# Inverting 32x32 instead of 16x16 diagonal blocks on GpSimd before the doubling on TensorE

## The reference

```python
A = jnp.where(strict_lo, kb @ jnp.swapaxes(k, -1, -2), 0.0)
Tinv = jax.scipy.linalg.solve_triangular(eye + A, eye, lower=True, unit_diagonal=True)
u = Tinv @ v
w = Tinv @ kb
def step(S, xs):
    q_i, k_i, u_i, w_i = xs
    attn = jnp.where(strict_up, 0.0, q_i @ jnp.swapaxes(k_i, -1, -2))
    u_i = u_i - w_i @ S
    o_i = q_i @ S + attn @ u_i
    S = S + jnp.swapaxes(k_i, -1, -2) @ u_i
    return (S, o_i)
```

## Time and profile before

| what | value |
|---|---|
| median of the runs | 3596.17 us |
| the profiled execution, its span | 3601.86 us, 3600.1 us |
| PE busy, share of the span | 3078.8 us, 86% |
| DVE busy | 2413.5 us, 67% |
| ACT busy | 1393.4 us, 39% |
| POOL busy | 383.3 us, 11% |
| mean granted clock of PE | 0.884 of full speed |
| ordinary step that starts at 1554.64 us | 206.80 us |

### The profile page before, as it was taken

The page is one execution under the profiler, slowest core; times in us unless marked ns, Lnnn a source line. Parts: engine busy times, 40 slices in busy tenths (PEclk is TensorE's granted clock), DMA queues, the critical chain, the costliest instruction groups (busy, mean ns, idle before and its releaser), DMA issues.

```text
span 3600.1 us, 49639 instructions
## 1 busy us (share of the span) xinstructions
PE 3078.8 (86%) x18500; PEld 2342.5 (65%) x18500; DVE 2413.5 (67%) x5735; ACT 1393.4 (39%) x2889; POOL 383.3 (11%) x710
## 2 busy tenths in 40 slices
PE   4689899898989889898998989889898989988565
PEld 2467767676766767676676767667676766757352
DVE  5436677686867668686766768585676858675754
ACT  2344343534444253434434343443434344332311
POOL 1001010010102011010100101020010101020200
PEclk7699889898989989898998989899898989988666
DMA  3344253323334232333424233432432353231100
GB/s 103 74 100 118 42 115 71 82 67 88 81 87 97 59 91 65 82 80 87 100 57 103 67 76 71 106 80 57 104 76 69 69 105 81 54 89 45 34 14 20
DMA packets 592814, 275.94 MB, mean 77 GB/s; under 512 B 464808, under 2 KB 555072, under 8 KB 592576
## 3 DMA queue, kind: packets, MB, share of 16 engines
q1 hardware_dynamic: 490176, 138.53, 20.3%
q10 hardware_dynamic: 102400, 134.23, 12.6%
HBM read 156.55 MB, written 14.68 MB: 48 GB/s over the span
## 4 chain that ended last, share of the span: by engine, by line
PE 53%; DVE 24%; issue 6%; ACT 6%; DMA 4%; POOL 4%; SPq 2%; DVEq 0%; POOLq 0%; ACTq 0%
PE bank L906 20%; PE bank L1111 7%; DVE region L2000 6%; PE bank L981 4%; PE bank L958 3%; PE bank L941 3%; PE bank L1272 2%; ACT pt_f L1371 2%; PE bank L915 2%; DMA qT_f<-pt_f 2%; DVE nm_f L1738 2%; POOL region L884 1%; PE bank L1239 1%; PE bank L1204 1%; SPq L716 1%
## 5 line engine op out<-in xcount | busy, mean ns | idle before, releaser
L906 PE MATMUL bank<-xTc,c_w 128*128 128x256 f32 x2048 | 528.4, 405 | 3.2 <-DVE yc L1924 3.1
L1371 ACT ACTIVATE pt_f<-bank 128x512 f32<-128x512 f32 x768 | 419.1, 597 | 266.0 <-PE bank L958 262.9
L1111 PE MATMUL bank<-c_w,c_hb 128*128 128x256 f32 x2048 | 481.9, 384 | 2.8 <-ACT c_hb L1504 2.4
L906 PEld LDWEIGHTS bank<-xTc,c_w 128*128 128x128 f32 x2048 | 403.1, 206 | 71.5 <-issue 7.3
L1738 DVE TENSOR_REDUCE nm_f<-bank 128x2 f32<-128x512 f32 x512 | 316.3, 685 | 164.3 <-PE bank L941 162.1
L2000 DVE SCALAR_TENSOR_TENSOR region<-vpad,cols,region 128x256 f32<-128x256 f32 x1024 | 420.2, 485 | 0.0
L1111 PEld LDWEIGHTS bank<-c_w,c_hb 128*128 128x128 f32 x2048 | 377.3, 191 | 64.8 <-issue 11.1
L958 PE MATMUL bank<-qT_f,kT_f 102*128 102x256 bf16 (+1 forms) x1536 | 275.7, 296 | 65.8 <-ACT pt_f L1371 33.7
L1504 ACT ACTIVATE c_hb<-bank,cols 128x256 f32<-128x256 f32 x512 | 213.6, 476 | 303.5 <-PE bank L906 302.5
L958 PEld LDWEIGHTS bank<-qT_f,kT_f 102*128 102x128 bf16 (+1 forms) x1536 | 129.1, 101 | 219.9 <-ACT pt_f L1371 98.4
L981 PE MATMUL bank<-pt_f,v_f 128*32 128x256 f32 x3072 | 219.9, 419 | 0.0
(11 more groups left out here) (317 smaller groups left out, 5140.9 us busy)
## 6 DMA issues: line engine op xcount, KB each, us to landing
c_w<-in_c_w ACTq DMA_DIRECT2D x256, 512.0 KB, 4.9
gram_scratch<-region SPq DMA_DIRECT2D x32, 256.0 KB, 2.2
x<-in_x SPq DMA_DIRECT2D x16, 256.0 KB, 2.7
x<-in_ctx SPq DMA_DIRECT2D x16, 256.0 KB, 2.9
ctxb<-in_ctx SPq DMA_DIRECT2D x16, 256.0 KB, 3.0
out_dram<-x SPq DMA_DIRECT2D x16, 256.0 KB, 2.4
qT_f<-split_f SPq DMA_TRANSPOSE x192, 3.4
kT_f<-split_f SPq DMA_TRANSPOSE x192, 3.4
```

Source lines behind the costliest of these rows:

```text
L906: mm = pe.matmul(out_ap, l, r, start=(i == 0), stop=(i == len(pairs) - 1))
L1111: mm = pe.matmul(PS[use][:, t * D:(t + 1) * D], c_hb[:, k, t * P:(t + 1) * P], c_w2[:, e % W_SLOTS, k, :], start=(k == 0), stop=(k == HC - 1))
L1371: act.activation(dst, PS[use].rearrange("p (c s) -> p c s", c=c), func, **kw).then_inc(*PS.drained(use))
```

## The change

`BASE` goes from 4 to 5. POOL inverts 32 blocks of 32x32 on 32 partitions, one column after the other (31 columns, so 62 `TENSOR_TENSOR` in place of 30), and segments `d_one4`, `d_two4` and `d_twb4` with their matmuls and DVE instructions no longer exist. The DMAs that gather and place blocks are 4 and 4 in place of 8 and 8, with twice the rows in each. `blkX` and its transposed inverse now lie over the tiles `uu` and `dd`, and `blk_tmp` lies in `wTn`. The order tables of PE, ACT and DVE are written anew for all steps.

```diff
-BASE = 4
+BASE = 5
...
-       + ["d_fir0", "d_place", "d_fir1", "d_fir2", "d_fir3"]
+       + ["d_fir0", "d_fir1", "d_place", "d_fir2", "d_fir3", "d_fir4"]
...
-b_score3a d_out b_score3b b_weigh2 b_weigh3 d_res b_out c_down7b b_res
+d_mix b_score0b b_score1a b_score1b b_weigh0 b_score2a c_down7a b_score2b b_weigh1 b_score3a d_out b_score3b b_weigh2
...
-        lev_mask = sb("lev_mask", [P, LEVELS - 1 - BASE, P])
+        lev_mask = sb("lev_mask", [P, 2, P])
...
-        low = region[0:P // 2, 2048:3072]
-        blkX, blkT, blkU = (low[:, i * 256:(i + 1) * 256].rearrange("p (r c) -> p r c", r=BB) for i in range(3))
-        blkT2 = low[:, 256:768]
-        blk_tmp = low[:, 768:832]
...
+        BN = 8 * NBK
+        square = lambda x: x[0:BN, 0:BB * BB].rearrange("p (r c) -> p r c", r=BB)
+        blkT, blkX = square(region[:, 2048:3072]), square(region[:, 3072 + 7 * 512:3072 + 9 * 512])
+        blkU = blkX
+        blk_tmp = wTn[0:BN].rearrange("p a s -> p (a s)")
...
-                    sp.dma_start(inv_dram[:, m], blkT2[:, m * 256:(m + 1) * 256]).then_inc(*d_inv_out.up)
+                    sp.dma_start(inv_dram[:, m], (blkT, blkU)[m].rearrange("p r c -> p (r c)")).then_inc(*d_inv_out.up)
...
-                    step(pool.tensor_tensor(tmp, blkX[:, j, j + 1:].unsqueeze(2).to_broadcast([P // 2, n_, m_]),
-                                            blkT[:, j, 0:m_].unsqueeze(1).to_broadcast([P // 2, n_, m_]), ALU.mult))
+                    step(pool.tensor_tensor(tmp, blkX[:, j, j + 1:].unsqueeze(2).to_broadcast([BN, n_, m_]),
+                                            blkT[:, j, 0:m_].unsqueeze(1).to_broadcast([BN, n_, m_]), ALU.mult))
```

More of the change, by code:

```diff
@@ L148 @@
[L148 to L151 removed]
+c_in d_in a_norm c_gate a_proj d_proj e_max0 c_comb e_max1 c_up0a e_max2 c_up0b e_max3 c_down0a c_down0b e_again
@@ new lines @@
+c_up1a c_up1b e_score0a c_down1a e_score0b e_score1a c_down1b e_score1b e_weigh0 e_score2a c_up2a e_score2b e_weigh1
+e_score3a d_token e_score3b e_weigh2 e_weigh3 a_v e_out c_up2b d_chan c_down2a c_down2b d_gram c_up3a f_in a_score0a
+d_grams a_score0b c_up3b f_up0 a_score1a c_down3a a_score1b c_down3b f_up1 c_up4a a_weigh0 a_score2a c_up4b a_score2b
+a_weigh1 a_score3a c_down4a a_score3b c_down4b f_round0 a_weigh2 a_weigh3 f_round1 c_up5a a_out b_in d_one5 b_ctx
+d_two5 a_res d_twb5 f_down d_one6 b_x c_up5b b_proj d_two6 c_down5a d_scan0 c_down5b c_up6a d_scan1 d_scan2 d_scan3
@@ L183 @@
+c_up7a c_up7b d_out c_down7a d_res c_down7b
 """),
     ("tensor", 17, """
[L185 to L188, removed]
+d_in d_proj d_token d_chan d_gram d_grams e_max0 e_max1 e_max2 e_max3 e_again e_score0a e_score0b e_score1a e_score1b
@@ L243 @@
     ("vector", 2, """
-a_norm c_gate a_proj a_rope c_comb d_proj d_conv a_part1 c_down0b d_silu a_part2 d_token c_down1b d_norm d_gram
-d_grams c_down2b c_down3b d_fir0 d_fir1 d_fir2 d_fir3 c_down4b d_one4 d_fir4 a_out b_ctx d_two4 a_res d_twb4 a_apply
-d_one5 d_fir5 b_proj d_two5 b_part1 c_down5b d_twb5 b_part2 d_fir6 d_sums b_max0 b_max1 d_turn b_max2 b_max3 b_shift
-d_logit c_down6b d_weight d_mix d_ms d_out d_res d_apply b_out c_down7b c_res c_apply b_res b_apply
+a_norm a_proj c_gate a_rope c_comb d_proj d_conv a_part1 c_down0b d_silu a_part2 d_token c_down1b d_norm d_gram
@@ L248 @@
+c_down2b d_grams d_fir0 d_fir1 c_down3b d_fir2 d_fir3 d_fir4 c_down4b a_out b_ctx a_res a_apply b_proj d_one5 b_part1
+d_fir5 d_two5 b_part2 d_twb5 d_fir6 d_sums c_down5b b_max0 b_max1 d_turn b_max2 b_max3 b_shift d_logit c_down6b
+d_weight d_mix d_ms d_out d_res b_out d_apply c_down7b c_res b_res c_apply b_apply
 """),
     ("vector", 16, """
-e_part1 e_part2 c_gate e_max0 e_max1 c_comb e_max2 e_max3 e_shift d_proj d_conv c_down0b d_silu d_token d_norm d_gram
-e_out e_res e_apply f_in c_down1b d_grams d_fir0 d_fir1 d_fir2 f_up0 d_fir3 c_down2b f_up1 f_round0 c_down3b f_round1
@@ L252 @@
-d_one4 d_fir4 d_two4 c_down4b d_twb4 d_one5 d_fir5 d_two5 d_twb5 d_fir6 d_sums d_turn c_down5b d_logit f_res d_weight
-f_apply d_mix d_ms c_down6b d_out d_res c_down7b d_apply c_res c_apply
+e_part1 e_part2 c_gate e_max0 e_max1 c_comb e_max2 d_proj e_max3 e_shift d_conv d_silu c_down0b d_token d_norm d_gram
+e_out e_res e_apply f_in d_grams c_down1b d_fir0 d_fir1 f_up0 d_fir2 d_fir3 c_down2b f_up1 f_round0 c_down3b f_round1
+d_fir4 c_down4b d_one5 d_fir5 d_two5 d_twb5 d_fir6 d_sums d_turn c_down5b d_logit f_res d_weight f_apply d_mix d_ms
@@ L254 @@
+c_down6b d_out d_res c_down7b d_apply c_res c_apply
 """),
     ("vector", 17, """
[L256 to L258 removed]
+d_proj e_part1 d_conv e_part2 d_silu d_token d_norm d_gram e_max0 e_max1 e_max2 e_max3 e_shift d_grams d_fir0 d_fir1
@@ L259 @@
+d_fir2 d_fir3 e_out e_res e_apply f_in d_fir4 f_up0 f_up1 f_round0 f_round1 d_one5 d_fir5 d_two5 d_twb5 d_fir6 d_sums
+f_res f_apply d_turn d_logit d_weight d_mix d_ms d_out d_res d_apply
 """),
```

98 lines of the change are left out of this document (47 added, 51 removed).

## The result

| | median | runs | profiled execution (span) |
|---|---|---|---|
| before | 3593.49 us | 4, 3589.05 to 3604.67 | 3601.86 (3600.1) |
| changed | 3773.51 us | 4, 3767.67 to 3781.53 | 3774.24 (3772.5) |

The ratio is 1.0498, 95% interval 1.0466 to 1.0529: the changed kernel is 5.0% slower.

What follows compares the result with a forecast made beforehand. PE sets the pace, DVE between `d_gram` and `d_one5`. Thirteen ordinary steps at 15.5 us (201.5), 16 for two batches, 18 for step 17 and 15 for stalls sum to 250: 3850 us against 3596, range 3700 to 3970.

Steps and rivals of the forecast that it cites:

- The direction and its cause: Whole kernel: slower, chance 0.92, because POOL's longer inversion makes PE wait at `d_one5` for `d_T0`.
- POOL's chain: POOL's inversion in layer d, first product to end of copy: 45 us, of which 36.5 undisturbed.
- the two roundings: DVE's roundings of layer f beside POOL's inversion: they slow POOL by 2 x 2.6 = 5.2 us.
- The other loss: DVE's taps beside POOL's inversion: some 16 us of them cost POOL 2.8 us.
- The path to `d_T0`: First Gram matmul to the waiting matmul of `d_one5`: 11.3 us, POOL's 45, then 7.3; 63.6 us.
- The low clock: PE after the wait at `d_one5`: matmuls at half the granted clock, about 2.3 us with what follows.
- The size of the wait: PE at `d_one5` in ordinary steps: reached near 1600 on the shown clock, then some 20 us waiting.
- the new placing of the other segments: Rewritten order of segments outside the removed level: priced at 0, with 3 us a step either way.
- The stalls: POOL's occasional 7 us product, in 4 batches of 16 before: about 7 expected, adding 15 us.
- the steps outside the ordinary ones: First and next to last batches of layer d, 16 us together, and step 17, 18 us.
- The last step: Step 17, layer e's norm behind POOL's inversion: `rstd` starts right behind the copy; 18 us more.
- Rival A: Wide POOL instructions cost hardly more, `d_T0` in time below about 30 us: 68 us gained, 3530; chance 0.06.

Runs made afterwards that it cites:

- e1: Changed kernel with POOL inverting only the upper left 16x16 of each 32x32 block (15 columns; output incomplete); 3501.2 us, ratio 0.9744.
- e5: e1 plus 40 powers on POOL ahead of the releasing copy, keeping POOL busy while hardly touching SBUF; 3805.5 us, ratio 1.0585.
- e6: e1 with its early release, then 50 unused POOL multiplications of the long chain's widths behind the copy; 3738.9 us, ratio 1.0408.
- e4: Changed kernel with `d_one5` in ordinary steps moved behind `b_ctx`, `a_res`, `f_down` on PE and behind `a_apply` on DVE; 3810.3 us, ratio 1.0608.
- e7: Changed kernel with the order tables of the kernel before, only the removed level's three segments struck; 3854.6 us, ratio 1.0702.
- e3: Kernel before with the changed kernel's order tables, the segments `d_one4`, `d_two4`, `d_twb4` put back; 3563.2 us, ratio 0.9905.

## Why the prediction came out as it did

- **The direction and its cause** were right: `d_one5` waits for the placing DMA in 15 of 16 batches, e1 shows that POOL's longer chain makes the whole loss, and e5 that its lateness is enough for it.
- **POOL's chain:** 45 us forecast, 45.1 to 45.7 in ordinary steps. Its parts hold too: 0.19 us and 1.7 ns an element give 0.61 us for 247 elements, where L885 took 0.59 beside L1925 and L887 0.66 behind it; under the two roundings 15 instructions took 13.84 us (from 1661.68 to 1675.52), where the rule has 8.6, so 5.3 us were lost for 5.2 forecast. (The other loss, 2.8 us for taps, is 2.7 by its own factors.) By the Trainium skill, "GPSIMD Engine Reference", Elementwise — side-by-side cycle accounting, an estimate is 5 us more; the trace goes with the rows.
- **The path to `d_T0`:** 63.6 us forecast, 64.1 on average over 13 steps. Ahead of POOL it was 10.3 for 11.3, behind the copy 8.5 for 7.3: the four placing DMAs took 4.3 us from their first issue to L1194 where eight had taken 5.3 (1175.87 to 1181.16 before), but from the copy's end to that issue it is now 4.7 us and was 3.0.
- **The low clock:** 3.44 us for `d_one5`, 3.78 in most steps, and 19.8 us from its start to the last level for 17.7: 2.1 where 2.3 was forecast.
- **The size of the wait was wrong:** near 20 us forecast, 7 to 12.5 measured. The prediction has DVE slowing POOL, and nothing for POOL slowing DVE, which is the larger effect (a tap takes 0.75 us for 0.40). PE comes to `d_one5` 54.6 us behind the Gram, where 41.8 were forecast; in e5, with DVE undisturbed, it is 44.5, and the wait 20 to 24 us. Here the wait covered that, so the error did not show in the time. Where no wait does, it decides: e6, and as far as shown e4.
- **The step that was mis-sized is "the new placing of the other segments I price at 0, with 3 us a step either way".** It brought 4 us a step, outside its own margin. Counted from Gram to Gram, twelve ordinary steps went from 207.4 (without the two that hold a 7 us product) to 219.1 us, +11.7 where the forecast had 15.5; that is 46 of the 78 us by which the profiled execution lies below 3852. The thirteenth such length, which ends in step 16, went from 193.4 to 210.2 us, +16.8. The gap is in the rest of the step, 141 us before and 135 after, where layers b and c lie. e7 shows it: with the old order the rest takes 142 us. The new placing stood in the diff, and I had priced only the 1.7 us by which `d_gram` comes earlier. Which of the moved segments brings it was not tried.
- **That e7 comes within 5 us of 3850 is partly luck:** the forecast takes off 22 us in 13 steps for the earlier `d_gram`, which e7 does not have, and adds 15 for stalls, of which e7 has one. The mechanism fits better than that number: without the 1.7 us the forecast is 17.2 us more for an ordinary step, and e7 has 224.7 for 207.4.
- **The stalls** made most of what is left, 27 us: I expected 7 for 4 and 15 us more; the changed kernel has none, which takes 12 us from the ordinary steps in place of adding (before, two of these lasted 213.3 and 213.7 us). POOL's first products there are 0.23 to 0.5 us. More instructions don't bring them: e3, with the very POOL code of before, has none either. In the one profiled execution of each, the kernels with the old order had them (4 in before, one of 8.79 us in e7), the seven with the new order had none. What they are stays open; "code arriving" was a guess. The last 5 us are the steps outside the ordinary ones, 27 us longer where 34 were forecast, less 1 us in the thirteenth length.
- **The last step:** the `rstd` of layer e starts right behind the copy, as forecast (3580.24, where the copy of 1.88 us started at 3578.38). The time from the last batch's first Gram to the end of the span went from 229.2 to 243.5 us, +14.3 for 18.
- **Rival A** had the gain right in size: with a chain of 14 us the kernel takes 3501, 62 below e3, for 68. Its condition, "below about 30 us", counts POOL's length alone, and not what wide instructions do to DVE; no chain between 14 and 45 us was run. And by the prediction's own terms (62 x 0.26 + 1.8 us) a chain of 29.5 us allows 1.1 ns an element, not 0.7; the 1.7 measured lies above both.

## What to carry to other kernels

Work that is moved to an idle engine can cost twice: by its length on the path, and by what it does to an engine that works beside it. Price both in the stretch where they lie. Where they run side by side, as here, the later of the two sets the time, not the sum; before moving the waiting instruction away, ask whether what stands ahead of it is slowed as well. When a change brings a new order of everything, the order is a change of its own: compare how the untouched part of the step is laid out, and count as free what the order puts ahead of a wait that ends last.

## What the runs showed that was not expected

DVE and POOL slow each other, and only for some operands. Beside POOL's wide products a tap (two inputs in SBUF) takes 0.75 us, and 0.40 once POOL is done. In the rounding, L1687 with two inputs takes 1.29 us and L1688 with a single one 0.79; in e1, with POOL idle, they are

```profile
1548.76 0.89 DVE L1687 TENSOR_TENSOR split_f<-split_f 128x704 f32<-128x704 f32 x1
1549.69 0.53 DVE L1688 TENSOR_SCALAR split_f<-split_f 128x704 uint32<-128x704 uint32 x1
```

L1925, which reads a bank, does not change. By the Trainium skill, "GPSIMD Engine Reference", Specifications, the two contend when DVE has two SBUF inputs or a two-port mode; the taps, L1687 and L1925 agree, and L1688 would have to be in such a mode, which no run here shows. By the Trainium skill, "SBUF — State Buffer", SBUF: two separate sides, the pair of ports is locked for a whole instruction and the other engine blocks. The rows do not agree with that. At the start of the long chain, in the first batch:

```profile
340.80 22.73 DVE L2001 SCALAR_TENSOR_TENSOR region<-vpad,cols,region 128x256 f32<-128x256 f32 x30
```

A tap each 0.76 us, while POOL starts an instruction each 0.7 to 0.9 us. If each locked the other out for the lengths in the rows, a tap (0.40 alone) and a product (0.6 alone) would take over 1.0 us together. It looks like one tap for one POOL instruction, and POOL instructions of other widths in the traces bear that out. In e6:

```profile
1643.87 8.06 DVE L2012 SCALAR_TENSOR_TENSOR region<-vpad,cols,region 128x256 f32<-128x256 f32 x10
```

Here the distance from one tap to the next falls from 0.83 to 0.76 us behind the first tap, and the distance between POOL's starts beside them as well, as its multiplications narrow from 240 to 207 elements. Over the rows of taps in the nine traces, the median distance between two taps and between two POOL starts beside them is 0.80 and 0.80 us at 247 elements, 0.72 and 0.72 at 192, 0.60 and 0.61 at 135, 0.48 and 0.48 at 87, and 0.40 and 0.40 at 39, where a tap has its undisturbed length and the two run beside each other (one behind the other would take at least 0.40 + 0.24 us). So in these runs taps go at POOL's pace as soon as POOL starts its instructions more than 0.40 us apart. Why is not shown.
